# One of seven block products moved to the end of its part, its operand built beside two others, and the edge DMAs of GpSimd spread out

## The reference, cut to what matters

```
xn = layernorm(x)                                        # [1250, 1024]
u = xn @ root + bias
for r in range(8):                                       # relations
    mask = (edge_type == r)
    sums = segment_sum(xn[src] * mask, dst)
    u += sums / max(count_r, 1) @ weight[r]              # weight [8, 1024, 1024]
z = concat([u, xn], 1) @ w_gate + b_gate
gnn = tanh(u) * z + xn * (1 - z)
q, k, v, g = xn @ Wq, xn @ Wk, xn @ Wv, xn @ Wg + bg     # 16 heads of 64
q, k, g = elu(q) + 1, elu(k) + 1, sigmoid(g)
mix = (q / 8 @ (k.T @ v) / (q . sum(k)) * g) @ Wo        # per head
x1 = x + gnn + mix
i, o, c = (layernorm(x1) @ W.T + b for W, b in ...)      # right halves of W_i, W_o, W_c
out = x1 + sigmoid(o) * tanh(sigmoid(i) * tanh(c))
```

## Time and profile before

| what | value |
|---|---|
| median of 3 runs | 2289.55 us |
| the profiled execution | 2288.27 us, span 2286.4 us |
| TensorE busy | 2143.4 us, 94% of the span |
| VectorE busy | 1361.2 us, 60% |
| GpSimd busy | 854.9 us, 37% |
| ScalarE busy | 513.7 us, 22% |
| mean granted TensorE clock | 0.968 |
| HBM read and written | 415.83 and 133.10 MB, 240 GB/s over the span |

### The profile page before, as it was taken

The page is one execution under the profiler, slowest core; times in us unless marked ns, Lnnn a source line. Parts: engine busy times, 40 slices in busy tenths (PEclk is TensorE's granted clock), DMA queues, the critical chain, the costliest instruction groups (busy, mean ns, idle before and its releaser), DMA issues.

```text
span 2286.4 us, 25382 instructions
## 1 busy us (share of the span) xinstructions
PE 2143.4 (94%) x9562; PEld 1723.3 (75%) x9562; DVE 1361.2 (60%) x1748; ACT 513.7 (22%) x713; POOL 854.9 (37%) x679
## 2 busy tenths in 40 slices
PE   7867599687999999999999999999999999999999
PEld 6655377566788777888887777778998887777887
DVE  5456279985666666656666657665346567734233
ACT  4323122222211111110012120011222222421121
POOL 3257521322455555554374645552121345000000
PEclk9988799898999999999999999999999999999999
DMA  7998366355858888878396878985348998613112
GB/s 280 322 332 290 104 223 210 121 181 185 301 161 299 297 302 290 301 276 287 113 330 235 301 268 280 302 272 182 115 138 231 271 313 283 172 51 119 45 56 77
DMA packets 253490, 509.57 MB, mean 223 GB/s; under 512 B 39665, under 2 KB 72096, under 8 KB 253366
## 3 DMA queue, kind: packets, MB, share of 16 engines
q1 hardware_dynamic: 171126, 291.08, 38.8%
q0 software_dynamic: 65248, 191.13, 25.4%
q10 hardware_dynamic: 16992, 25.73, 3.5%
HBM read 415.83 MB, written 133.10 MB: 240 GB/s over the span
## 4 chain that ended last, share of the span: by engine, by line
PE 74%; DMA 1%; issue 0%; DVE 0%; SPq 0%; POOL 0%; ACT 0%; DVEq 0%; ACTq 0%
PE acc L1404 68%; PE acc L1399 5%; PE acc L1312 1%; PE misc L1297 1%; DMA aTraw<-ax_d 0%; PE acc L1412 0%; POOL slot_d L2357 0%; SPq L1010 0%; DMA slot_d<-table,slot 0%; PE misc L1312 0%; DVE res L1732 0%; ACT L1512 0%; ACT aThi L1460 0%; DVE Wlo L1678 0%; DVE res L1985 0%
## 5 line engine op out<-in xcount | busy, mean ns | idle before, releaser
L1404 PE MATMUL acc<-Whi,aThi 128*128 128x512 f32 (+1 forms) x2232 | 882.9, 396 | 5.6 <-issue 5.6
L1404 PE MATMUL acc<-Whi,aTlo 128*128 128x512 f32 (+1 forms) x2232 | 879.8, 394 | 0.0
L1404 PE MATMUL acc<-Wlo,aThi 128*128 128x512 f32 (+1 forms) x2232 | 877.3, 393 | 0.0
L2370 POOL DMA_INDIRECT ring<-y_d,edge x390 | 489.4, 1255 | 438.3 <-DVE U L1958 157.1
L1404 PEld LDWEIGHTS acc<-Whi,aThi 128*128 128x128 f32 (+1 forms) x2232 | 414.1, 186 | 108.0 <-issue 6.0
L1404 PEld LDWEIGHTS acc<-Wlo,aThi 128*128 128x128 f32 (+1 forms) x2232 | 415.0, 186 | 102.7
L1404 PEld LDWEIGHTS acc<-Whi,aTlo 128*128 128x128 f32 (+1 forms) x2232 | 414.1, 186 | 103.6
L1678 DVE TENSOR_TENSOR Wlo<-Wraw,Whi 128x1024 fp32r<-128x1024 f32 x176 | 235.2, 1341 | 243.0 <-ACT Whi L1430 242.0
L1375 PE MATMUL acc<-Whi,aThi 128*128 128x512 f32 (+2 forms) x560 | 239.3, 427 | 116.3 <-DVE Wlo L1678 31.5
L1958 DVE SCALAR_TENSOR_TENSOR U<-ring,edge,U 128x1024 f32<-128x1024 f32 x180 | 230.3, 1279 | 25.4 <-DMA ring<-y_d,edge 25.0
L1430 ACT CAST Whi<-Wraw 128x1024 fp32r<-128x1024 f32 x176 | 183.0, 1044 | 251.5 <-POOL Wraw L2319 70.4
(11 more groups left out here) (202 smaller groups left out, 1567.4 us busy)
## 6 DMA issues: line engine op xcount, KB each, us to landing
Wraw<-in_L_gnn_weight SPq DMA_DIRECT2D x88, 512.0 KB, 7.6
Whraw<-in_L_gnn_weight SPq DMA_DIRECT2D x40, 512.0 KB, 7.0
y_d<-res SPq DMA_DIRECT2D x80, 256.0 KB, 2.5
y_d<-made ACTq DMA_DIRECT2D x32, 256.0 KB
Wraw<-in_L_gnn_w_gate SPq DMA_DIRECT2D x16, 512.0 KB, 8.1
y_d<-made ACTq DMA_DIRECT2D x32, 252.0 KB
ring<-y_d,edge POOLq DMA_INDIRECT x390, 6.2
aTraw<-ax_d SPq DMA_DIRECT2D x4, 1250.0 KB, 11.5
```

The source lines that it names most:

```text
L1404: mm = nc.tensor.matmul(to, a[:, k, rows(i)], b[:, s % 2, k, :], start=start, stop=stop)
L2370: pool.indirect_dma_start(ring[:, j % RING, :], None, a, bass.IndirectOffsetOnAxis(ap=index, axis=0), bounds_check=top - 1, oob_is_err=Fal ...
```

## The change

The four stages BE, GA for each relation now follow the four AL stages at once, and the two DE stages come last. T4 is made in every BE stage by one more sum per half: T3 in Wraw, T2 = B11 + T3 in Wraw, T4 = B21 + T2 in Whraw; B21 is loaded there with B22. SyncE stores T4 to t4_d, and the DE stages load it as a plain granule. BE's second product is stored where DE's was, by ScalarE; DE's eviction subtracts the stored block from its bank (`evict_less`), and VectorE's second subtraction per BE unit goes. The left sums are made in place and spread to the slots by four splits in SBUF (`hi_spread`, `lo_spread`, table SPREAD); as_d goes, and the four reloads that are left bring the raw blocks back. The edge steps lie five units earlier (280 becomes 240), run reads are written down two per unit from unit 49, sends one per unit, both edge loads at unit 141. In units 0 to 139 SyncE writes weight loads down first of a unit in place of last.

```diff
-STAGE = [(AL_, r, 0) for r in SEVEN] + [(DE_, r, 0) for r in SEVEN[::2]]
-STAGE += [(k, r, 0) for r in SEVEN for k in (BE_, GA_)]
+STAGE = [(AL_, r, 0) for r in SEVEN] + [(k, r, 0) for r in SEVEN for k in (BE_, GA_)]
+STAGE += [(DE_, r, 0) for r in SEVEN[::2]]
...
+SPREAD = [(3, 0, POS[AL_LAST, 4], 35), (3, 3, 0, 37), (2, 1, LAST[AL_LAST], 41), (2, 2, 0, 43)]
...
-SUM_BESIDE = {DE_: (-2, -2, 0, 0, 2, 2, 3, 3, 5, 5, 8, 8), BE_: (2, 2, 3, 4), GA_: (-1, 0)}
+SUM_ORDER = {BE_: [(0, 1), (1, 1), (0, 2), (1, 2), (0, 3), (1, 3)], GA_: [(0, 1), (1, 1)]}
+SUM_BESIDE = {BE_: (2, 2, 3, 4, 5, 6), GA_: (-1, 0)}
...
-LOAD_AT = {LAST[0] + 1: list(range(2 * GRAN, 3 * GRAN))}
+LOAD_AT = {POS[0, 4] + 1: [2 * GRAN, 2 * GRAN + 1], LAST[0] + 1: [2 * GRAN + 2, 2 * GRAN + 3]}
...
+    if STAGE[_s][0] == BE_:
+        FOUR_AT[FIRST[_s - 1] + 7], FOUR_AT[FIRST[_s - 1] + 8] = (_s, 0), (_s, 1)
...
-    return divmod(280 + (8 * (q - 17) + k) * 13 // 8, 8)
+    return divmod(240 + (8 * (q - 17) + k) * 13 // 8, 8)
...
                 elif kind == DE_:
-                    fetch(Wraw, quarter(r + g // 2, 0, 0, g % 2))
-                    fetch(Whraw, quarter(r + g // 2, 0, 1, g % 2))
+                    sp.wait_ge(t4_st[g % 2], 16 * (r + g // 2 + 1))
+                    fetch(Wraw, t4_d[r + g // 2][g % 2 * 256:g % 2 * 256 + 256, :])
...
                     fetch(Wraw, quarter(r, 1, 1, g - 2))
+                    if kind == BE_:
+                        fetch(Whraw, quarter(r, 1, 0, g - 2))
...
+            def store_four(s, p):
+
+                r = STAGE[s][1]
+                sp.wait_ge(w_sum, sums_to(s, p, 3))
+                sp.dma_start(t4_d[r][p * 256:p * 256 + 256, :].rearrange("(b p) n -> p b n", p=128),
+                             granule(Whraw, GRAN * s + 2 + p)).then_inc(t4_st[p], 16)
...
-                    if q == edge_at(61, 0)[0]:
+                    if q == BLOCK_UNITS + 1:
                         load_edges(0)
-                    if q == edge_at(76, 0)[0]:
                         load_edges(1)
...
                 if kind == BE_:
-                    act.wait_ge(w_sum, sums_to(s, g, 2) if g < 2 else sums_to(s, g - 2, 1))
+                    act.wait_ge(w_sum, sums_to(s, g % 2, 2))
+                    if g >= 2:
+                        act.wait_ge(t4_st[g % 2], 16 * (STAGE[s][1] + 1))
...
+            def hi_spread(j):
+
+                of, to, after, _ = SPREAD[j]
+                act.wait_ge(right_made, 4)
+                if of == to:
+                    act.wait_ge(a_lo, j)
+                else:
+                    act.wait_ge(prod, after + 1)
+                (k, n), (own, cols) = left(of), left(to)
+                a = aTraw if of == to else aThraw
+                nc.scalar.copy(aThi[:, own, cols], a[:, k, n]).then_inc(a_hi, 1)
...
-                if STAGE[s][0] == BE_ and g >= 2:
-                    dve.wait_ge(w_sum, sums_to(s, g - 2, 2))
+                if STAGE[s][0] == BE_:
+                    dve.wait_ge(w_sum, sums_to(s, g % 2, 3))
...
                 nc.vector.tensor_tensor(kept(q), kept(q), bank(q), ALU.subtract).then_inc(evac_v, 1)
+
+            def evict_less(q):
+
                 wait_part(dve, q)
-                nc.vector.tensor_tensor(made_in(q), made_in(q), bank(q), ALU.subtract).then_inc(evac_v, 1)
+                dve.wait_ge(prod, q + 1)
+                nc.vector.tensor_tensor(made_in(q), bank(q), made_in(q), ALU.subtract).then_inc(evac_v, 1)
...
-                if q == edge_at(28, 2)[0]:
+                reads = q - edge_at(READS_AT, 0)[0]
+                if reads == 0:
...
-                    for i in range(2):
-                        for t in range(T):
-                            read_run(i, t)
+                if 0 <= reads < T:
+                    for i in range(2):
+                        read_run(i, reads)
```

226 lines of the change are left out of this document (104 added, 122 removed).

## The result

The changed kernel takes 2231.86 us (median of 3 runs, 2231.67 to 2237.38), the kernel before 2289.55. The ratio is 0.9764, 95% interval 0.9730 to 0.9798. It is faster, by 57.7 us where 116.6 were forecast; the time lies in the range of 2135 to 2240, near its slow end. The profiled execution took 2231.86 us for a span of 2230.0.

A forecast was written before the change was run, and what follows sets the result against it. TensorE bounds the kernel, so only its waits and low clock before unit 140 can be won, VectorE deciding in the ranking. 77.3 + 68 + 92.7 + 174 + 52 = 464 us, plus 1706.7 and 1.9: 2173 us; range 2135 to 2240.

The forecast's parts named there:

- Units 19 to 39: Stretch forecast at 68 us, between 58.5 (all hidden) and 93.0 (all stays), since bytes and matmuls need about the same.
- The 4 us for late x tiles: Units 19 to 39: allowance for the last two x tiles, whose loads wait for stores in the same queue.
- Unit 40: First seeded stage: seeds' loads wait in SyncE's queue behind stores; 4 us taken, between 0 and 21.66.
- The clock: Seven-product part: a unit that waits for nothing priced at 2.784 us; units 40 to 68 as 29 x 2.784 + 4 + 8.
- Unit 60: Reads among T4's sums make a chain of 35.5 us where 27.8 are free: 8 us wait, for 21.66 before.
- Units 69 to 121: Ranking of edges: VectorE decides; 177 - 10 + 7 = 174 us, for 201 before; bounds 147.6 and 201.
- may end four units behind: Units 69 to 121: VectorE may lag TensorE at the end, taking 10 us off, as the part's end is light.
- Units 122 to 139: T4 products: 50.1 us needed, 52 taken; each unit loads and stores a 256 KB block through SyncE, under 200 GB/s.
- T4's waits: Rival: seeded stages pay 31.5 us of split waits again, and half the ranking's 27 us stay: 2218 us, chance 0.18.
- The spread reads: Rival: spreading does not do what it says; 14 reads end 14 us later than counted: 2187 us, chance 0.06.
- VectorE did bind: Answers the rival that VectorE does not bind: ranking hides, all waits but 8 us go: 2131 us, chance 0.11.
- the slow case: Rival, slower than before: late T4 stores stop all banks through ScalarE's queue, 35 us a stage: 2313 us, chance 0.04.

The follow-up runs named there:

- fewer rounds: Three rounds instead of five of each node's edge search, against the changed kernel with T4 part loads one unit later and table weights in four pieces: 2208.06 us, ratio 0.9647.
- The first experiment: The later load: SyncE loads a T4 unit's part one unit later, against the changed kernel; 2224.13 us, ratio 0.9707 to the kernel before.

## Why the prediction was half right

*What bounds.* Right: all of the gain lies ahead of unit 140, and behind it nothing changed but 3.2 us. The direction and the waits that go (unit 19, unit 110, the edge check) came as written.

*Units 19 to 39.* The number is right, in part by luck: unit 19 waits for nothing, and unit 39 ends at 145.5 us, 67.9 behind the start of unit 19 where 68 stood. The 4 us for late x tiles are there, as two waits of 2.01 and 2.43 us inside unit 20. The other 5 or 6 stood for bytes, and these do not hold TensorE: units 19 to 22, then 23 to 39,

```profile
77.61:98.04 20.43, 15.99 (x66) 12.46 (x64) 14.04 (x21) 8.29 (x15) 4.75 (x2) 0.83 0.95 355
98.04:145.55 47.51, 47.51 (x205) 37.59 (x203) 21.02 (x12) 15.20 (x20) 5.40 (x3) 1.00 0.96 312
```

show it busy without a gap at clock 1.00 beside DMA engines at 0.96. What is left over 58.5 and the two waits lies in units 19 to 22, in transposes of x tiles and a clock of 0.83.

*Unit 40.* The step "I take 4, about a store and a load of such a block" failed. It is 14.8 us. The waits that I had read of the kernel before left out its 11.88 us at the same unit, for a weight split. I had looked for it in SyncE's order, T4 stores among seeds; it is the landing of the weights for the first sums, 18 us behind their issue with the DMA engines 0.92 busy. Whether these or SyncE's queue make them late stays open. The term for units 19 to 39 had the engines at 0.95 and drew from it how long these units take, but not how late the next stage's loads land.

*The clock.* The sum prices every unit at the 2.784 us of a clock of 1.00, and puts a lower clock at nothing, without a reason. In units 40 to 68 TensorE is busy 89.53 us, at 0.89, where 29 x 2.784 are 80.7: 8.8 of the 12.8 us that this stretch is over.

*Unit 60.* The chain was priced rightly (8 us; 5.9 and 2.9 waited), the step behind it was not: VectorE's wait for the last reads holds the splits of unit 65, 3 us. I had let only evictions stand behind it.

*Units 69 to 121.* VectorE binds, as forecast: 174.48 us busy where 172.8 stood. Wrong is the 10 us for which VectorE "may end four units behind": TensorE can lag so on an eviction, but most of its waits here are for splits, of which it has none in hand. The stretch is VectorE's busy time and 8 to 10 us in four kernels (204.13 for 194.75, 184.02 for 174.48, 183.37 for 173.73, 178.32 for 169.84); with fewer rounds it is 17.2.

*Units 122 to 139.* The step that failed most, 22.3 us: each unit's load and store were priced by their bytes, "under 200 GB/s", and not by the landing that SyncE's queue waits for in every unit. The bytes were no hindrance: all traffic of the stretch was 186 GB/s, and 239 with the later load. The first experiment gives 13.7 of the 22.3 (74.3 to 60.6) to the loop in SyncE's queue; some 9 stay, with parts and stores behind a left block, and are open.

*The rivals.* None of them, as written, is what happened. T4's waits came back for some 11 us, not 45; TensorE's waits for weight splits as a whole did not shrink (40.1 us in the changed kernel, 31.5 in the earlier trace rows), so that rival saw where the time would go, but not what would hold the splits. The spread reads did end late, at unit 65. VectorE did bind, and the slow case is far: none of ScalarE's waits between 140 and 446 us ends in one of T4's stores. The range, which was to take in the second to the fourth time, ends at 2135, above the 2131 of the second; that did not matter here.

## What to carry to other kernels

For a stage that loads and stores a small block per step, write down which landing each load waits for and which store stands behind that load in the same queue: a loop through one landing bounds the step by latency, whatever the bandwidth, and one place of distance may break it. Where engines run near full, ask of each long wait in front of an operand split (not only of an eviction) what stands behind it in the same queue; moving one piece out of the way only pays if the chain that ends next is shorter. An engine that binds in a dense stretch and idles in the next is helped by spreading its work, with not one instruction less. And where the DMA engines are as busy as here (0.92) and the issuing queue is as full, don't price the next stage's loads by the median landing of the whole part: 18 us stood here for 7.8. Last, price a stretch with waits in it at the clock that its rows show, not at the full one.
